# Scatters tied to the exponentials of their step, and filler products of 512 columns in the stages without experts

## The reference, cut to what matters

```python
xn  = layernorm(x)
out = x + attention(xn) + experts(xn)

# attention: 16 heads of size 8, causal
q, k, v = split(xn @ w_qkv)
p  = softmax(where(causal, q @ k.T * 8**-0.5, -inf))
attention = (p @ v) @ w_proj + b_proj

# experts: 8, each token uses its 2 best, weights from a softmax over the two logits
h  = gelu(xn @ W1[e] + b1[e])        # 128 -> 512
o  = h @ W2[e] + b2[e]               # 512 -> 128
experts = sum over the two experts of gate * o
```

## Time and profile before

| | |
|---|---|
| median of 3 runs | 870.83 us (866.7 to 873.35) |
| profiled execution, own time | 874.43 us |
| its span, first to last instruction | 872.7 us |
| TensorE, matmul busy | 740.8 us (85%) |
| VectorE busy | 557.2 us (64%) |
| ScalarE busy | 449.5 us (52%) |
| GpSimd busy | 283.1 us (32%) |
| mean granted TensorE clock | 0.842 of full |

### The profile page before, as it was taken

How to read it: one execution, slowest core, us unless ns; L and a number is a source line. 1 busy time by engine, 2 the same in 40 slices (tenths; PEclk the granted TensorE clock), 3 DMA queues, 4 the chain that set the end, 5 groups by cost and what they waited for, 6 DMA issues and landing times.

```text
span 872.7 us, 15135 instructions
## 1 busy us (share of the span) xinstructions
PE 740.8 (85%) x5021; PEld 420.3 (48%) x5021; DVE 557.2 (64%) x2164; ACT 449.5 (52%) x717; POOL 283.1 (32%) x454
## 2 busy tenths in 40 slices
PE   3683779986788989888898999889998989899995
PEld 2562434432345554544555555545545555555543
DVE  4749535554576666767667666756676766667656
ACT  2212123233355566655656665646566666666663
POOL 7103841573502333323132322222242323141421
PEclk9555555567797799999799989989799999898997
DMA  6997310210239051523425250605234342430074
GB/s 154 166 154 257 116 40 13 70 47 23 68 78 273 16 159 43 148 77 103 115 71 140 57 147 18 193 29 133 86 92 118 87 118 83 142 107 5 22 180 120
DMA packets 96261, 88.74 MB, mean 102 GB/s; under 512 B 8368, under 2 KB 83672, under 8 KB 96184
## 3 DMA queue, kind: packets, MB, share of 16 engines
q1 hardware_dynamic: 91432, 78.05, 34.6%
q0 software_dynamic: 4544, 9.35, 3.3%
q10 hardware_dynamic: 208, 0.38, 0.2%
HBM read 50.18 MB, written 21.32 MB: 82 GB/s over the span
## 4 chain that ended last, share of the span: by engine, by line
PE 64%; DVE 19%; issue 4%; SPq 4%; DMA 3%; ACT 3%; POOL 2%; another core or an unknown queue 2%; DVEq 0%; ACTq 0%; POOLq 0%
PE ov L773 18%; PE aux L741 15%; PE aux L831 10%; PE aux L783 6%; DVE maxes L963 5%; DVE junk L964 3%; SPq L444 3%; PE sc L695 3%; PE aux L788 2%; DMA hid<-in_L_ffn_W 2%; PE sc L696 2%; PE sc L697 2%; DVE maxes L959 2%; DVE xrow L1017 2%
## 5 line engine op out<-in xcount | busy, mean ns | idle before, releaser
L648 ACT ACTIVATE probs<-sc 128x1024 f32<-128x1024 f32 (+3 forms) x384 | 295.4, 810 | 254.5 <-PE sc L759 241.3
L741 PE MATMUL aux<-kT,qT 32*128 32x512 f32 (+3 forms) x768 | 244.6, 483 | 79.4 <-DVE maxes L964 22.6
L561 POOL TENSOR_SCALAR_AFFINE_SELECT probs<-probs 128x256 f32<-128x256 f32 x256 | 103.8, 409 | 422.7 <-ACT probs L648 418.7
L963 DVE TENSOR_REDUCE maxes<-aux 128x1 f32<-128x128 f32 (+2 forms) x384 | 161.1, 420 | 70.9 <-PE aux L741 64.3
L959 DVE TENSOR_REDUCE maxes<-aux 128x1 f32<-128x512 f32 x256 | 163.4, 684 | 60.1 <-PE aux L741 54.3
L741 PEld LDWEIGHTS aux<-kT,qT 32*128 32x128 f32 x768 | 108.3, 205 | 193.6 <-DVE maxes L964 52.7
L773 PE MATMUL ov<-probs,v 128*32 128x512 f32 (+3 forms) x1536 | 187.9, 565 | 2.4 <-POOL probs L561 2.3
L759 PE MATMUL sc<-qT,kT 32*128 32x512 f32 (+3 forms) x768 | 170.6, 465 | 4.2 <-DMA qT<-mT 2.7
L964 DVE CUSTOM_DVE_ANT_0 junk<-aux,cst 128x128 f32<-128x128 f32 x512 | 140.7, 282 | 19.3 <-PE aux L741 18.1
L586 POOL DMA_INDIRECT ys<-ysb,back x78 | 76.0, 974 | 77.4 <-issue 46.3
L831 PEld LDWEIGHTS aux<-w2b,hid 128*128 128x128 f32 x624 | 78.6, 197 | 41.8 <-DVE maxes L964 28.8
(11 more groups left out here) (117 smaller groups left out, 647.4 us busy)
## 6 DMA issues: line engine op xcount, KB each, us to landing
w1b<-w_scr SPq DMA_DIRECT2D x39, 512.0 KB, 4.3
w2b<-in_L_ffn_W SPq DMA_DIRECT2D x39, 256.0 KB, 3.5
xs<-ysb SPq DMA_DIRECT2D x6, 838.5 KB, 19.0
xrow<-in_L_attn_x SPq DMA_DIRECT2D x8, 512.0 KB, 6.6
kT<-kqh SPq DMA_DIRECT2D x32, 128.0 KB, 2.8
qT<-kqh SPq DMA_DIRECT2D x32, 128.0 KB, 2.7
w_scr<-w1b SPq DMA_DIRECT2D x8, 512.0 KB
xsin<-xs SPq DMA_DIRECT2D x9, 387.0 KB
```

Source lines behind the costliest of these rows:

```text
L561: nc.gpsimd.affine_select(out=block_, in_=block_, compare_op=ALU.is_ge, fill=0.0, base=0, pattern=[[0, 2], [1, P]], channel_multiplier=-1) ...
L648: nc.scalar.activation(probs[:, s % 2, 2 * half:2 * half + 2, 0:cols], pair(part)[:, :, 0:cols], ACT.Exp).then_inc(sc_done, 1)
L741: nc.tensor.matmul(bank(part)[:, 0:cols], qT[n % 3][rows, P * i:P * i + P], kT[n % 3][rows, k0:k0 + cols], start=True, stop=True).then_inc ...
L963: nc.vector.reduce_max(maxes[:, i, other, h:h + 1], bank(part)[:, 0:cols - P], axis=AX.X)
```

## The change

Three things change. The filler parts are kept only in stages without experts (0, 1, 2 and 15), so the 22 in stages 3 to 14 go. A filler part is now four products (WARM = 4) of 512 columns in the one-pass float32r format, of a weight tile with token data, where it was three of 128 columns in float32. And each scatter of stages 0 and 1 now waits until ScalarE has finished the last exponential that stands before it in the list (PACED); the first four, ahead of stage 0, don't.

```diff
@@ unit_parts
-        if not any(x[0] in full_array for x in parts[here:]):
+        if f is None and not any(x[0] in full_array for x in parts[here:]):
             parts.append(("warm", n, s))
@@
-WARM = 3
+WARM = 4
@@
+PACED = {x: [y for y in SCHED[:i] if y[0] == "scores"][-1] for i, x in enumerate(SCHED)
+         if x[0] == "scatter" and any(y[0] == "scores" for y in SCHED[:i])}
@@ GpSimd
                 elif what == "scatter":
                     t, k = part[1:]
+                    if part in PACED:
+                        pool.wait_ge(sc_done, PAIRI[PACED[part]] + 1)
@@ TensorE, part "warm"
                     if unit:
                         aux_free(unit)
+                        moving = xh if part[1] < FFN_UNIT[0] else xsh
                         for _ in range(WARM):
-                            nc.tensor.matmul(bank(unit)[:, 0:P], ident, upper, start=True, stop=True)
+                            nc.tensor.matmul(bank(unit)[:, :], wh[:, 0:P], moving[:, 0:W], start=True, stop=True)
```

## The result

The changed kernel takes 867.6 us in the median of 20 runs (860.02 to 874.41), against 872.76 us in 20 runs of the kernel before beside them (866.7 to 878.86). The ratio is 0.9945 with a 95% interval of 0.9921 to 0.997: half a per cent faster, where 834 us and 4% were forecast, and 9.6 us above the range's upper end of 858. The profiled execution of the changed kernel took 861.4 us by its own time, 6 us under the median. Ratios and intervals here leave out the few executions that were over 1.5% above the fastest of their kernel, medians count all of them.

What follows compares the result with a forecast made beforehand. TensorE was taken to bound stages with experts, with a low clock and two stalls in the early stages. Terms -9.9 - 22.5 + 10.6 - 20 + 5 = -36.8 us took the median 870.8 to 834 us, range 812 to 858.

Steps and rivals of the forecast that it cites:

- Pacing, -9.9 us: stages 0 and 1: scatters waiting for their step remove two pieces without an engine, -9.9 us, bounds 0 and -13.1.
- R3: rival, stages 0 and 1: the stalls have another cause than the run of scatters; 844 us, chance 10%.
- the two stalls: stages 0 and 1: chain pieces of 3.87 and 9.19 us without an engine, each late in twelve back-to-back scatters.
- Filler out of stages 3 to 14: stages 3 to 14: removing 22 fillers, 26.5 us in the chain, gives -22.5 us, bounds -26.5 and -18.
- its clock term: stages 3 to 14: 11 us more at the lower clock level without filler, +5 us, bounds -5 and +27.
- prediction's own price of 0.45: each us at the lower clock level costs 0.45 us, read from two expert stages of like content.
- The recovery of 85%: stages 3 to 14: 85% of the removed fillers' 26.5 us comes back, read from stage 5.
- R2: rival, stages 3 to 14: clock falls without filler; mild: 50 us more low, costing 22 us, 10%; slower form, 6%.
- Longer filler, +10.6: stages 0 to 2 and 15: the fourth product costs 0.43 or 0.22 us per filler, +10.6 us in all.
- the clock of stages 0 to 2, -20: stages 0 to 2: longer filler moves 45 us to the upper clock level, -20 us, bounds 0 and -40.
- R1: rival, stages 0 to 2: the longer filler does not raise the clock, stage 0 near 0.54; 854 us, 17%.
- R4: rival, stages 0 and 1: scatters among VectorE's work get slow, +60 us, 894 us, chance 1%.

Runs made afterwards that it cites:

- 873 us kind: series of runs on one chip in which the kernel before took 873.97, 873.22 or 874.33 us.
- e8: kernel before with the long filler in stages 0 to 2 and 15, the old one in 3 to 14, no pacing: ratio 0.9996.
- e1: kernel before with only the 22 fillers of stages 3 to 14 left out: ratio 1.0037, 3.2 us slower.
- e9: kernel before, word for word, profiled beside e10; the kernel before took 873.22 us in that series.
- e13: the changed kernel again, word for word, in another series: ratio 1.0056 to the kernel before, 862.7 us.
- e5: kernel before with pacing, and in stages 3 to 14 the old filler kept at step 1 only: ratio 0.9891.
- e3: changed kernel with the old filler back in stages 3 to 14: ratio 0.9873 to the kernel before, 866.95 us.
- e2: kernel before with the pacing alone: ratio 0.987.
- e4: changed kernel with its long filler in stages 3 to 14 too: ratio 0.9891 to the kernel before, 866.52 us.
- e10: kernel before with the pacing alone, same kernel as e2 in another series: ratio 0.9875.
- e17: kernel before with the pacing alone, same kernel as e2 and e10 in another series: ratio 0.9878.
- 859 us kind: series of runs on one chip in which the kernel before took 859.32 or 858.08 us.
- e6: as e5, but the filler at step 1 of stages 3 to 14 is the long one: ratio 0.9986 to the kernel before.
- e18: same kernel as e12 in another series: 838.69 us, ratio 0.9608 to the kernel before.
- e12: kernel before with pacing, no filler in stages 0 to 2, old filler at step 1 only in stages 3 to 14: 846.16 us, 0.969.
- e11: kernel before with only the 26 fillers of stages 0 to 2 left out, no pacing: ratio 0.9858.

## Why the prediction was wrong, point by point

**Pacing, -9.9 us: right**, in the 873 us kind of series. Measured alone: -11.4, -10.9 and -10.7. The piece by piece working gave the size, and no cost of the waits shows. What the prediction could not see is that the standstills depend on more than the run of scatters. R3 as it was put, that the pacing does nothing, is out for these series; in the others nothing was lost to a standstill in the unpaced e8, and what the pacing alone does there was not run. The prediction's remark that the clock was at 0.50 around the two stalls because nothing ran has no support: it had been at 0.50 for 19 and 9 us before they began (from 102.2 and 184.1 us), with matmuls in work.

**Filler out of stages 3 to 14 and its clock term, -22.5 + 5 = -17.5 us: wrong**, and this is most of the miss. The edit alone measured +3.2 us (e1), 21 us off. The step that failed is these two terms, the clock term first: it took 11 us more at the lower level, and it was 48 (75 to 123 us). At the prediction's own price of 0.45 that is 21.5 us in place of 5. The recovery of 85% was read from stage 5, to the end of the select, where the products ahead of the values product end later at the lower level; half came back at that place (0.8 of 1.6 us). The profile shows +8.4 us for both terms (551.0 to 559.4), in place of -17.5; the timed +3.2 of e1 lies below it, as does e1's own profile (556.0 with 112.6 us low).

How much of this belongs to each term isn't settled, because the price is too high. The prediction read it from stages 7 and 10 as of like content. In e9, the same kernel, both have the same time at the lower level, and stage 10 is still 0.7 us the longer:

```profile
475.19:518.79 43.60, 40.26 (x311) 22.37 (x310) 30.33 (x123) 28.43 (x45) 12.43 (x23) 0.96 0.38 104
618.01:662.32 44.31, 40.95 (x314) 23.17 (x314) 30.38 (x122) 28.01 (x44) 14.30 (x25) 0.96 0.36 101
```

Stage 10 set against itself, 44.3 us with 3.4 low and 46.5 with 10.2, gives 0.33 us per us. Stages 3 to 14 as a whole give 0.35 and 0.36: 545.1 us with 58.0 low in e9 and 551.1 with 75.1 in the kernel before, 552.0 with 102.4 in e13 and 559.4 with 122.9 in the changed kernel. By 0.45 the 48 us cost 21.5 us and 13 of the 26.5 us of filler came back; by 0.35 they cost 17 and only 8 or 9 came back. Either way both terms were too favourable.

R2's mild form, 50 us more at 22 us, had the clock almost exactly. It was given 10%. The argument against R2 was that ten of the 22 fillers ran at the lower level anyway. It counts the other way: those ten are all at step 1, and with the filler there the low stretch ends earlier, as the low times of e1 and e5 show. The prediction also had the fall in the thin steps 10, 11 and 0, at the end of a stage, and asked whether the filler of step 10 stops it. In the kernel before steps 3 to 11 of stages 3 to 14 have next to no time at the lower level (0.1 us in all); each of the twelve falls lies between 0.1 us before and 2.5 us after the first exponentials of a stage. The filler at step 1 comes behind the fall and shortens what follows it.

The stages that seemed to speak against R2, 6 and 10, lack the filler of step 10, which is indeed worth nothing; every stage from 3 to 14 of the kernel before has the one at step 1, so its worth could not be read there.

The idle rule of the Trainium skill (TensorE: Matmul & The Clock Gate, section "HAM oscillation — how this bites in real kernels") would have made this term 0. The windows of stage 5 above are against it: TensorE had a matmul in work for 11.44 of 11.98 us at 0.57, and for 9.04 of 10.18 us, with more idle time, at 0.83. Keeping the term was right and its size was not.

**Longer filler, +10.6, and the clock of stages 0 to 2, -20: the clock rose, the time didn't follow.** The chain of the changed kernel prices the filler as forecast, 1.58 + 0.43 = 2.01 us at the lower level:

```profile
97.72 2.00 PE aux L791 x4
...
105.68 2.01 PE aux L791 x4
```

and stages 0 to 2 took 174.8 us, 21.8 us fewer, against a forecast of -9.9 + 8.6 - 20 = -21.3. Stage 0 at 0.69 and 73.6 us is near what was said for "right". This agreement was luck of one profile, as is shown below. And timed, the long form against the short one gives nothing: e3 against e2 (0.9873, 0.987) and e8 against the kernel before (0.9996). By the sum it should have been -9.4 us. This is R1 in its effect on the time, for another reason: in this profile the clock did rise.

Besides the changed kernel's, three more profiles have its code of stages 0 to 2. Here are these stages of e4, e13 and e3:

```profile
85.25:263.99 178.74, 151.11 (x799) 70.59 (x798) 108.42 (x440) 69.66 (x105) 86.97 (x119) 0.78 0.30 90
...
86.63:267.81 181.18, 155.82 (x797) 71.74 (x796) 106.86 (x436) 69.93 (x105) 86.96 (x119) 0.74 0.29 88
...
85.97:276.32 190.35, 163.41 (x797) 75.25 (x797) 107.53 (x438) 69.98 (x106) 87.00 (x119) 0.71 0.28 84
```

and e5, of e13's kind of series, with pacing and the short filler:

```profile
85.44:260.64 175.20, 148.80 (x849) 75.21 (x848) 108.29 (x440) 69.77 (x106) 87.20 (x119) 0.75 0.30 88
```

So the changed kernel's 174.8 us at 0.81 is the best of four. In the 873 us kind the long filler has 174.8, 178.7 and 190.3 us against 185.2, 189.1 and 190.9 with the short one (e2, e10, e17), 7 us less in the mean. In the 859 us kind it has 181.2 us with 94 us low, against 175.2 and 175.7 us with 88 us low (e5, e6): there it neither raised the clock nor saved time. The term of -20 us had no row behind it. With the filler's own +8.6 us it should have shown as -11 us in these stages, and the profiles have -7 in one kind of series and +6 in the other.

The deeper fault is one the prediction shares with both kernels: it asked what a longer filler brings beyond the old one, and never what the old one costs. Without filler stages 0 to 2 have 135 to 149 us at the lower level (e18, e12) and take 168.4 and 171.5 us, less than in any other kernel of the 873 us series. Between e10 and e12, of one series, they shrink by 17.6 us although 20 us more are at the lower level. As an estimate, by a price of 0.35 to 0.45 that is 7 to 9 us of clock given up for some 24 to 27 us of filler, about 1.0 us for each of the 26. Against the changed kernel's 67 us at the lower level the 68 to 82 us more would be worth 24 to 37 us at that price, and its longer fillers eat it. No run prices the clock in these stages by itself.

**The sum.** Single effects, each timed alone or as a pair: pacing -11, filler out of stages 3 to 14 +3, longer filler 0, together -8 us. The change itself measured -5 (-0.55%), and +5 (e13) where the pacing has nothing to free, against +3 by these parts; so they add up to within 3 us in both kinds, and the forecast's -36.8 missed by 21 us in stages 3 to 14 and by 9 in stages 0 to 2 and 15. **R4** is out: no scatter took over 1.24 us.

## What to carry to other kernels

A filler that nothing reads paid here only where the low stretch ended earlier with it, at step 1 of stages 3 to 14, and not at step 10, nor in stages 0 to 2, which stay low for most of their time in any case. Ask of each filler separately, and of the old ones first, what the same stretch would take without it; a higher granted clock is no gain until the stretch is shorter. And before a per-microsecond price is applied, find the place at which the clock rises and what stands just ahead of it.

## What the runs showed of the hardware

- ScalarE, in stage 0 with VectorE, stands still with its inputs ready late in a run of twelve indirect DMAs issued by GpSimd (5.79 and 6.58 us above; 3 to 9 us in the chains of four profiles without pacing). Mostly it goes on after GpSimd has written the last of them, 1.4 and 2.1 us in e9 (124.22 to 125.58, 201.09 to 203.19) and 2.3 us both times in the kernel before, but in e11 while the tenth was written (119.30). In the series where the kernel before took 859 us the one unpaced kernel profiled, e8, didn't show it. What sets this isn't known; the chip that bore number 12 had a series of either kind (858.08 and 874.33 us).
- A matmul in work nearly all the time did not bring TensorE's clock up: in the changed kernel it was granted 0.50 from 358.1 to 368.3 us, and a matmul was in work for 9.78 of the 10.00 us from 358.2.
- A microsecond at the lower level cost about a third of a microsecond in stages 3 to 14, where TensorE shares the time with waits for VectorE (stage 10: 44.3 us with 3.4 low, 46.5 with 10.2).
- Stage 0 at the lower level throughout, without filler, took 66.6 us in both e12 and e18.
